# Conditioning stage of a two-layer kernel: work moved from GpSimd and VectorE to ScalarE, output rows accumulated by DMA, last batch reordered

## The chip, the cores and the metric

One core of a Trainium2 chip runs the whole program. The metric is device time in microseconds of one execution, as the median of several runs. Below, PE is TensorE, DVE is VectorE, ACT is ScalarE, POOL is GpSimd and SP is SyncE, which only issues DMAs.

## The reference, cut to what matters

Eight batches of 512 tokens with 256 channels, all in float32.

```python
# layer 0: adapter + layer norm, 8 experts that each choose 128 tokens of a batch; then x = x + layer0
# layer 1, conditioning of every batch (E = 256 channels, D = 8 time constants):
ctx    = causal_ema(x, tau_ctx)                       # h = alpha*h + b over the tokens
gated  = x * sigmoid([x, ctx] @ Wg.T + bg)
mod    = 0.5 + sigmoid(gelu(x @ Wn1.T + bn1) @ Wn2.T + bn2)
traces = causal_ema(gated * mod_d, tau_d) for d in 0..7
temporal = sum_d traces_d * softmax(blend)_d
gate   = sigmoid(temporal @ Wtemp.T + btemp)
soma   = gelu(x @ Wsoma.T + bsoma)
z      = layernorm((soma * gate) @ Wout.T) * gamma + beta
# layer 1, feed-forward on z:
probs  = softmax(z @ router.T)                        # 64 experts, top 8, weights divided by their sum
routed = sum over the chosen experts of weight * (silu(z@Wg_e) * (z@Wu_e)) @ Wd_e   # 128 slots each
shared = (silu(z@Wsg) * (z@Wsu)) @ Wsd
out    = x + routed + shared
```

## The kernel before, in words

Each engine runs its own program, and the engines wait for each other on counting semaphores. `level(m)` is the count at which item m is done. The order on each engine is written out by hand.

Up to about 520 us the kernel does layer 0. Its POOL adds the results, row by row with indirect DMAs, into a DRAM tensor `x1_rows` that began as a copy of x. From 520 us to about 855 us it runs the conditioning as a pipeline over the batches: `conditioning` calls `step(b)` for b from -1 to 9. Step b works on the traces of batch b, on the gate, the output product and the layer norm of batch b-1 and on the routing and the shared feed-forward of batch b-2, and prepares batch b+1. From about 857 us the 64 routed experts follow.

The units that the change and the prediction touch:

- `weighted(b, d)` (ACT) scales the gated input by a blend weight; `drive_of(b, d)` (POOL, L635) multiplies it by the modulation; `scan_unit(b, d)` (DVE, L1271) runs the moving average over it; `add_trace(b, d)` adds the result to a sum, on POOL (L643) for d = 1, 2, 3, 5, 6, 7 and on DVE (L1280) for d = 4 (and for d = 6, 7 of the last batch). There are three drive buffers and three trace buffers.
- `temp_in` (PE), `gate_out` (ACT, L936), `gate_soma` (DVE) and `out_in` (PE, L1714) follow on the finished sum. `stats` (DVE) takes mean and variance, `rstd_of` (POOL, L621 to L626) makes the scale and shift, `normalise` (ACT, L945) writes four tiles of `zrow`, and `z_in` (PE, L1722) transposes them.
- On PE a step is: `x1T_in(b+1)`, `shared_b_in(b-2)`, `logits_in(b-2)`, `h1_in(b+1)`, `temp_in(b-1)`, `shared_a_in(b-2)`, `t8_in(b+1)`, `out_in(b-1)`, `wg_in(b+1)`, `down_in(b-2)`, `z_in(b-1)`, `soma_in(b+1)`.
- `pick` (DVE) finds the eight largest logits, and writes the mask `mask_all` (L1335). `route_weights` (DVE) divides the chosen exponentials by their sum and puts them behind the 256 channels in `zrow`. `z_store` (SP) writes `zrow` to `z_rows`.
- `shared_b`, `shared_a`, `down_in` are the shared feed-forward. `finish` (DVE, L1370) halves it and adds x, which `row_in` (SP) has loaded from `x1_rows`; `row_store` (SP, L454) writes `out`.
- `prep(k, part)` turns `mask_all` into the token numbers (`slots`, L1409) of experts 4k to 4k+3. Experts 0 to 3 are prepared in `last_share`, that is, in step 9.
- In the expert stage POOL issues for each expert a gather of 128 rows of `z_rows` (L721) and a scatter that adds 128 result rows to `out` or `odd_rows` (L728), all in one order. At the end one DMA adds `odd_rows` to `out` (L745).
- `turn(n, count)` (PE, L1601) multiplies constants into an unused PSUM bank.

## Time and profile before

| | us |
|---|---|
| median of 3 runs | 1121.03 |
| lowest and highest run | 1117.95, 1122.76 |
| the profiled execution, its own time | 1116.69 |
| its span, first to last instruction | 1114.9 |
| layer 0 | 0 to about 520 |
| conditioning, batches 0 to 7 | about 520 to 856 |
| routed experts | about 857 to 1091 |
| last accumulation of `odd_rows` | 1091 to 1115 |

Over the span PE is busy 86%, DVE 67%, ACT 41% and POOL 60%. A share of busy time is an average over stages that have different limits, so the stages have to be read one by one. The profiled execution was 4.3 us faster than the median.

### The profile page before, as it was taken

How to read it: one execution, taken by the hardware profiler on the slowest of the kernel's cores; microseconds unless marked ns; L12 is line 12 of the kernel's file. 1: busy time of each engine (PE TensorE's matmuls, PEld its weight loads, DVE VectorE, ACT ScalarE, POOL GpSimd, SP SyncE). 2: the span in 40 equal slices, each digit the busy share in tenths (PEclk: the TensorE clock that was granted, in tenths of full speed). 3: DMA queues.
4: the chain of work that ended last, by engine and by line, in shares of the span. 5: the costliest groups of instructions: out<-in, count | busy, mean ns of one | idle time of the engine just before them, and what ended most of it. 6: DMA issues, size and time to landing. Idle time of an engine off the chain costs nothing.

```text
span 1114.9 us, 14811 instructions
## 1 busy us (share of the span) xinstructions
PE 954.6 (86%) x4524; PEld 668.5 (60%) x4524; DVE 743.1 (67%) x1522; ACT 461.2 (41%) x835; POOL 664.1 (60%) x496
## 2 busy tenths in 40 slices
PE   4968999999999999987379899988586899999960
PEld 2533698899989998863144555544353565556640
DVE  3648566667666766524779999999955786777620
ACT  1330444554455545533455665666421232222320
POOL 2113444555455544407999999999931477777870
PEclk9989999999999999988689999999887799999995
DMA  5869234444354432223212752335168599997557
GB/s 174 281 231 352 58 76 118 90 87 99 76 122 90 92 88 39 30 85 76 96 66 70 240 157 86 91 118 182 44 229 274 143 270 256 257 262 150 91 75 157
DMA packets 89782, 155.46 MB, mean 139 GB/s; under 512 B 12072, under 2 KB 70128, under 8 KB 86576
## 3 DMA queue, kind: packets, MB, share of 16 engines
q1 hardware_dynamic: 48112, 91.27, 25.2%
q0 software_dynamic: 25104, 39.86, 20.6%
q10 hardware_dynamic: 16496, 23.49, 6.2%
q8 instruction: 32, 0.52, 0.2%
q14 instruction: 38, 0.31, 0.1%
HBM read 119.56 MB, written 43.42 MB: 146 GB/s over the span
## 4 chain that ended last, share of the span: by engine, by line
POOL 13%; PE 10%; issue 10%; DMA 9%; DVE 4%; ACT 2%; POOLq 2%; DVEq 1%; ACTq 0%; SPq 0%
DMA odd_rows<-ys,slots 5%; POOL wide L635 4%; PE bank L1662 4%; POOL wide L643 3%; DMA xg<-z_rows,slots 2%; POOL xg L721 2%; POOL out L728 2%; POOL odd_rows L728 2%; DVE wide L1271 1%; PE bank L1739 1%; PE bank L1729 1%; PE bank L1722 1%; ACT zrow L945 1%; DMA z_rows<-zrow 1%; ACT wide L895 1%
## 5 line engine op out<-in xcount | busy, mean ns | idle before, releaser
L635 POOL TENSOR_TENSOR wide<-wide 128x1024 f32<-128x1024 f32 x64 | 156.6, 2461 | 30.8 <-issue 30.6
L1271 DVE TENSOR_TENSOR_SCAN wide<-bank,wide 128x512 f32<-128x512 f32 x128 | 149.3, 1209 | 22.8 <-POOL wide L635 22.6
L871 ACT ACTIVATE h_raw<-bank,b 128x512 f32<-128x512 f32 x128 | 88.1, 689 | 168.1 <-PE bank L1635 165.7
L1208 DVE TENSOR_TENSOR h_lo<-h_raw,h_hi 128x512 fp32r<-128x512 f32 x128 | 87.3, 692 | 91.8 <-ACT h_hi L875 91.8
L1650 PE MATMUL bank<-w_hi,h_hi 128*128 128x256 f32 x512 | 144.4, 282 | 0.1
L1650 PE MATMUL bank<-w_lo,h_hi 128*128 128x256 f32 x512 | 142.1, 278 | 0.0
L1650 PE MATMUL bank<-w_hi,h_lo 128*128 128x256 f32 x512 | 142.0, 277 | 0.0
L609 POOL DMA_INDIRECT x_rows<-ob,put x64 | 110.3, 1723 | 28.3 <-issue 16.0
L643 POOL TENSOR_TENSOR wide<-wide 128x1024 f32<-128x1024 f32 x46 | 108.5, 2359 | 11.9 <-issue 8.1
L895 ACT ACTIVATE wide<-wide,blend 128x512 f32<-128x512 f32 x128 | 84.2, 715 | 59.3 <-POOL wide L635 55.5
L1635 PE MATMUL bank<-ex_hi,w_hi 128*128 128x512 f32 x256 | 99.5, 389 | 2.4 <-issue 2.4
L1635 PE MATMUL bank<-ex_hi,w_lo 128*128 128x512 f32 x256 | 100.8, 394 | 0.0
L1635 PE MATMUL bank<-ex_lo,w_hi 128*128 128x512 f32 x256 | 100.4, 392 | 0.0
L1650 PEld LDWEIGHTS bank<-w_hi,h_hi 128*128 128x128 f32 x512 | 96.9, 189 | 1.6 <-issue 1.1
L721 POOL DMA_INDIRECT xg<-z_rows,slots x64 | 63.5, 993 | 57.0 <-DMA z_rows<-zrow 25.9
L1650 PEld LDWEIGHTS bank<-w_lo,h_hi 128*128 128x128 f32 x512 | 96.9, 189 | 0.3 <-issue 0.2
L1650 PEld LDWEIGHTS bank<-w_hi,h_lo 128*128 128x128 f32 x512 | 96.7, 189 | 0.0
L603 POOL COPY put<-idxT 128x4 int32<-128x4 int32 (+1 forms) x16 | 3.0, 187 | 132.2 <-DVE ob L1197 132.2
L589 POOL DMA_INDIRECT xg<-n_rows,take x60 | 64.4, 1074 | 26.1 <-issue 13.7
L875 ACT ACTIVATE h_hi<-h_raw 128x512 fp32r<-128x512 f32 x128 | 77.9, 621 | 0.0
L728 POOL DMA_INDIRECT odd_rows<-ys,slots x32 | 51.4, 1606 | 20.0 <-DMA odd_rows<-ys,slots 9.7
L1042 ACT ACTIVATE sg<-bank 128x192 f32<-128x192 f32 x64 | 21.2, 331 | 100.4 <-PE bank L1887 100.4
(239 smaller groups left out, 2041.3 us busy)
## 6 DMA issues: line engine op xcount, KB each, us to landing
wide<-in_mwp SPq DMA_DIRECT2D x40, 512.0 KB, 4.5
wide<-m_rows SPq DMA_DIRECT2D x16, 1024.0 KB, 4.9
w1s<-in_fW SPq DMA_DIRECT2D x8, 1024.0 KB, 5.4
w2s<-in_fW SPq DMA_DIRECT2D x8, 1024.0 KB, 5.3
own<-in_mwp SPq DMA_DIRECT2D x15, 512.0 KB, 4.4
z_rows<-zrow SPq DMA_DIRECT2D x8, 640.0 KB, 7.4
head<-in_mwp SPq DMA_DIRECT2D x9, 512.0 KB, 4.5
xT<-in_xT ACTq DMA_DIRECT2D x8, 512.0 KB, 4.2
```

The lines of the kernel that those rows point to most:

```text
L609: G.indirect_dma_start(x1_rows[:, :], bass.IndirectOffsetOnAxis(ap=put[p][:, j:j + 1], axis=0), ob[p][:, j, :], None, compute_op=ALU.add). ...
L635: G.tensor_tensor(drive[n % DRIVES], gb[d % 2], md[d // HD][:, d % HD, :].unsqueeze(1).to_broadcast([P, CT, S]), ALU.mult).then_inc(c_u, 1)
L643: G.tensor_tensor(acc[b % 2][:, :, :], acc[b % 2][:, :, :], trace[((D - 1) * b + d - 1) % TRACES], ALU.add).then_inc(c_add, 1)
L721: G.indirect_dma_start(xg1[i][:, :], None, z_rows[:, :], bass.IndirectOffsetOnAxis(ap=slots[:, e:e + 1], axis=0)).then_inc(e_got[i], 16)
L728: G.indirect_dma_start((out, odd_rows)[e % 2][:, :], bass.IndirectOffsetOnAxis(ap=slots[:, e:e + 1], axis=0), ys[e % 6][:, :], None, compu ...
L871: A.activation(h1_raw[f % 4][:, :], bank[:, 2 + f % 4, :], ACT.Gelu_apprx_tanh, bias=b1_0[:, bass.ds(e, 1), f]).then_inc(b_h, 1)
L875: A.activation(h1_hi[:, f - 1, :], h1_raw[(f - 1) % 4][:, :], ACT.Copy).then_inc(b_hi, 1)
L895: o = A.activation(gb[d % 2][:, c, :], gated2[b % 2][:, c, :], ACT.Copy, scale=blend[:, c, d:d + 1])
L1208: V.tensor_tensor(h1_lo[:, f, :], h1_raw[f % 4][:, :], h1_hi[:, f, :].bitcast(F32), ALU.subtract).then_inc(b_lo, 1)
L1271: o = V.tensor_tensor_scan(dst[:, c, :], decay[:, d:d + 1].to_broadcast([P, S]), drive[(D * b + d) % DRIVES][:, c, :], 0.0, ALU.mult, ALU.add)
L1635: o = T.matmul(bank[:, 2 + f % 4, :], w[q][:, at], x[p][:, c, :], start=(c == 0 and n == 0), stop=(c == CT - 1 and n == 2))
L1650: o = T.matmul(rows4(6)[:, j, :], x[:, f, rows], w[q][:, f * H:(f + 1) * H], start=(f == 0 and n == 0), stop=(f == FT0 - 1 and n == 2))
```

## The change

Eight things are done. (1) x and the results of layer 0 are now put into `out` itself; the shared part is added to it by an accumulating DMA that POOL issues (`rows_add`), so that `row_in`, `row_store` and the load of x are gone. The halving of the shared part moves from DVE (`finish`) to ACT (`share_out`). (2) Traces 3 and 5 are added on DVE to traces 4 and 6 (`pair_traces`), and POOL adds the pairs; POOL has five adds for a batch, not six, and DVE two, not one. (3) Two small operations of `rstd_of` move to ACT (`moments`). (4) For all batches but the last, the mask is made by two ACT operations (`chosen_out`). (5) `route_weights` no longer divides; it stores the reciprocal as one more column of `z_rows` (324 columns now, not 320), and the expert stage multiplies. (6) The last batch's rows of `z_rows` go in two transfers from POOL (`last_rows`), first the 256 channels, then the 68 others. (7) In `last_share` the slots of experts 0 to 3 come ahead of the shared feed-forward. (8) PE runs `turn` at three places of the last two steps.

```diff
-ZW = H + E1
+ZW = H + E1 + 4
+        PAIRED = (4, 6)
+        SUMS = tuple(d for d in range(1, D) if d + 1 not in PAIRED)
@@ SP: row_in, row_store and their calls removed; c_load reads out, not x1_rows @@
@@ POOL @@
             def rstd_of(q):
-                pool.wait_ge(c_mv, level(q))
+                pool.wait_ge(c_mw, level(q))
                 pool.wait_ge(c_no, level(q - 1, TT))
-                G.tensor_scalar(veps1[:, :], mv1[:, :, 1], 4 * EPS, None, ALU.add)
-                G.tensor_scalar(shift1[:, :], mv1[:, :, 0], -1.0, None, ALU.mult)
-                pool.drain()
+            def last_rows(part):
+                pool.dma_start(z_rows[(B - 1) * S:TOK, part].rearrange("(t p) c -> p t c", p=P), zrow[:, :, part]).then_inc(z_last, 16)
+            def rows_add(q):
+                pool.wait_ge(c_fin, level(q))
+                pool.dma_start(out[q * S:(q + 1) * S, :].rearrange("(t p) c -> p t c", p=P), ost[:, :, :],
+                               accum_op=ALU.add).then_inc(c_ost, 16)
...
             for e in range(ROWS):
                 e_gather(e)
-            pool.wait_ge(c_ost, level(B - 1, 16))
+            rows_add(B - 1)
+            wait_moved(pool, c_ost, B - 1, 16)
@@ ACT @@
+            def moments(q):
+                act.wait_ge(c_mv, level(q))
+                act.wait_ge(c_no, level(q - 1, TT))
+                A.activation(veps1[:, :], mv1[:, :, 1], ACT.Copy, bias=4 * EPS)
+                A.activation(shift1[:, :], mv1[:, :, 0], ACT.Copy, scale=-1.0).then_inc(c_mw, 1)
+            def chosen_out(q):
+                act.wait_ge(c_top, level(q))
+                A.activation(rep[:, :, :], rep[:, :, :], ACT.Sign, bias=far[:, :], scale=-1.0)
+                act.drain()
+                A.activation(mask_all[:, :, q * TT:(q + 1) * TT].rearrange("p e t -> p t e"), rep[:, :, :], ACT.Relu).then_inc(c_ma, 1)
+            def share_out(q):
+                act.wait_ge(c_dm, level(q))
+                wait_moved(act, c_ost, q - 1, 16)
+                A.activation(ost[:, :, :], rows4(down_bank(q)), ACT.Copy, scale=0.5).then_inc(c_fin, 1)
                 if ahead(b + 1):
                     wg_out(b + 1)
+                if on(b - 2):
+                    share_out(b - 2)
                 if on(b - 1):
                     normalise(b - 1)
@@ DVE @@
+            def pair_traces(b, d):
+                n = (D - 1) * b + d - 1
+                dve.drain()
+                V.tensor_tensor(trace[n % TRACES], trace[n % TRACES], trace[(n - 1) % TRACES], ALU.add).then_inc(c_pair, 1)
+                dve.drain()
@@ last_share, DVE @@
                 pick(B - 1)
-                shared_b(B - 1)
                 prep(0, 1)
                 route_weights(B - 1)
                 prep(0, 2)
-                shared_a(B - 1)
+                shared_b(B - 1)
                 prep(0, 3)
                 prep(1, 0)
-                finish(B - 1)
+                shared_a(B - 1)
                 prep(1, 1)
@@ PE @@
                 down_in(B - 2)
+                turn(6, 2)
                 z_in(B - 1)
             def last_share():
+                turn(1, 2)
                 logits_in(B - 1)
                 shared_b_in(B - 1)
+                turn(1, 2)
                 prep(0, 0)
```

First place: ACT's instructions at the end of a step in the middle of the conditioning, before. L895 is `weighted`, L918 to L924 `t8_out`, L907 `wg_out`, L945 `normalise`, L952 `z_out`.

```order
L895 ACTIVATE wide<-wide,blend 128x512 x2
L918 ACTIVATE wide<-bank,bn_h 8x512
L921 ACTIVATE wide<-wide 8x512
L924 DMA m_rows<-wide 8x512
L895 ACTIVATE wide<-wide,blend 128x512 x2
L907 ACTIVATE bank<-bank,bg_h 128x512 x2
L945 ACTIVATE zrow<-bank,shift_b,rstd_b 128x256 x4
L895 ACTIVATE wide<-wide,blend 128x512 x4
L952 ACTIVATE zT<-bank,bet,gam 128x512 x2
```

The same place after (L903 is `weighted`, L950 and L951 `moments`, L915 `wg_out`, L993 `share_out`, L959 `normalise`, L966 `z_out`):

```order
L903 ACTIVATE wide<-wide,blend 128x512 x2
L926 ACTIVATE wide<-bank,bn_h 8x512
L929 ACTIVATE wide<-wide 8x512
L932 DMA m_rows<-wide 8x512
L903 ACTIVATE wide<-wide,blend 128x512 x2
L950 ACTIVATE veps<-mv_b 128x4
L951 ACTIVATE shift_b<-mv_b 128x4
L915 ACTIVATE bank<-bank,bg_h 128x512 x2
L993 ACTIVATE ost<-bank 128x1024
L959 ACTIVATE zrow<-bank,shift_b,rstd_b 128x256 x4
L903 ACTIVATE wide<-wide,blend 128x512 x4
L966 ACTIVATE zT<-bank,bet,gam 128x512 x2
```

`moments` stands ahead of `wg_out`, and `share_out`, which waits for `down_in`, stands between `wg_out` and `normalise`.

Second place: POOL's whole period in the middle of the conditioning, before. L635 is `drive_of`, L643 `add_trace`, L621 to L626 `rstd_of`.

```order
L621 TENSOR_SCALAR veps<-mv_b 128x4
L622 TENSOR_SCALAR shift_b<-mv_b 128x4
L624 TENSOR_TENSOR rstd_b<-veps,mhalf 128x4
L626 TENSOR_TENSOR shift_b<-shift_b,rstd_b 128x4
L635 TENSOR_TENSOR wide<-wide 128x1024
L643 TENSOR_TENSOR wide<-wide 128x1024
L635 TENSOR_TENSOR wide<-wide 128x1024 x2
L643 TENSOR_TENSOR wide<-wide 128x1024 x2
L635 TENSOR_TENSOR wide<-wide 128x1024
L643 TENSOR_TENSOR wide<-wide 128x1024
L635 TENSOR_TENSOR wide<-wide 128x1024 x2
L643 TENSOR_TENSOR wide<-wide 128x1024 x2
```

The same after (L626 is `drive_of`, L637 `add_trace`, L615 and L617 `rstd_of`, L644 `rows_add`), from `rstd_of` to the last add of the period:

```order
L615 TENSOR_TENSOR rstd_b<-veps,mhalf 128x4
L617 TENSOR_TENSOR shift_b<-shift_b,rstd_b 128x4
L626 TENSOR_TENSOR wide<-wide 128x1024 x2
L644 DMA out<-ost 128x4x256
L626 TENSOR_TENSOR wide<-wide 128x1024
L637 TENSOR_TENSOR wide<-wide 128x1024 x2
L626 TENSOR_TENSOR wide<-wide 128x1024
L637 TENSOR_TENSOR wide<-wide 128x1024
L626 TENSOR_TENSOR wide<-wide 128x1024 x2
L637 TENSOR_TENSOR wide<-wide 128x1024
L626 TENSOR_TENSOR wide<-wide 128x1024 x2
L637 TENSOR_TENSOR wide<-wide 128x1024
```

An add and two small operations are gone, and a DMA issue is new; the add of trace 4 stands right ahead of the next `rstd_of`.

Third place: POOL between the last batch's statistics and the first scatter, after (L640 is `last_rows`, L728 the gathers, L735 a scatter). Before, the gathers stood alone, behind a wait for SP's transfers.

```order
L617 TENSOR_TENSOR shift_b<-shift_b,rstd_b 128x4
L640 DMA z_rows<-zrow 128x4x256
L644 DMA out<-ost 128x4x256
L640 DMA z_rows<-zrow 128x4x68
L728 DMA xg_0<-z_rows,slots 128x324
...
L728 DMA xg_5<-z_rows,slots 128x324
L644 DMA out<-ost 128x4x256
L728 DMA xg_0<-z_rows,slots 128x324
L728 DMA xg_1<-z_rows,slots 128x324
L735 DMA out<-ys,slots 4224x256
```

The last `rows_add`, and the wait for its landing, stand behind six gathers and ahead of the seventh and of the first scatter.

## Rows read from the trace of the kernel before

**Rows 1.** Busy time of each engine in two stretches; PEclk is the granted clock's share.

```profile
core 0: us, PE busy (x) PEld busy (x) DVE busy (x) ACT busy (x) POOL busy (x), PEclk, DMA share, GB/s
604.40:641.60 37.20, 34.41 (x115) 19.18 (x114) 35.41 (x54) 23.89 (x38) 35.81 (x19) 0.95 0.65 197
...
820.00:850.00 30.00, 25.35 (x86) 15.12 (x84) 14.46 (x42) 6.57 (x12) 2.73 (x8) 0.83 1.00 341
```

**Rows 2.** Chain that ended last, one period: start, length, what.

```profile
609.31 4.84 POOL wide L635 x2
...
618.06 1.48 ACT zrow L945 x3
...
639.04 2.36 POOL wide L635
```

**Rows 3.** PE: `z_in` of batches 0 and 5 (timeline), and its waits from 604 to 754 us.

```profile
581.95 1.97 PE L1722 MATMUL bank<-ident,zrow 128*128 128x128 f32 x8 [4.93 <-ACT zrow L945]
...
768.86 1.09 PE L1722 MATMUL bank<-ident,zrow 128*128 128x128 f32 x8 [1.72 <-ACT zrow L945]
...
PE bank L1722 <- ACT zrow L945: 9.3, 4, 2.6
```

**Rows 4.** ACT timeline: `normalise`, `weighted` and a copy from PSUM.

```profile
654.68 1.93 ACT L945 ACTIVATE zrow<-bank,shift_b,rstd_b 128x256 f32<-128x256 f32 x4 [2.27 <-POOL shift_b L626]
656.50 2.56 ACT L895 ACTIVATE wide<-wide,blend 128x512 f32<-128x512 f32 x4
...
665.30 1.02 ACT L902 ACTIVATE head<-bank 128x1024 f32<-128x1024 f32 x1
```

**Rows 5.** POOL timeline: drives, a small operation and an add.

```profile
572.24 5.63 POOL L635 TENSOR_TENSOR wide<-wide 128x1024 f32<-128x1024 f32 x2
577.85 0.24 POOL L621 TENSOR_SCALAR veps<-mv_b 128x4 f32<-128x4 f32 x1
...
656.67 2.38 POOL L643 TENSOR_TENSOR wide<-wide 128x1024 f32<-128x1024 f32 x1 [0.16 <-issue]
...
771.39 4.67 POOL L635 TENSOR_TENSOR wide<-wide 128x1024 f32<-128x1024 f32 x2
```

**Rows 6.** DVE timeline: an add of two traces beside a POOL instruction.

```profile
572.46 3.21 DVE L1280 TENSOR_TENSOR wide<-wide 128x1024 f32<-128x1024 f32 x1 [0.40 <-POOL wide L643]
```

**Rows 7.** POOL's direct accumulating DMA, and landing times of `row_store` (L454).

```profile
1090.71 1.16 POOL L745 DMA_DIRECT2D out<-odd_rows  x1 [2.71 <-DMA odd_rows<-ys,slots]
...
DMA to landing us min/median/max: 2.9/3.7/10.2
```

**Rows 8.** PE in the last batch: windows, its logits, and `turn` in layer 0.

```profile
834.00:835.00 1.00, 0.00 (x0) 0.00 (x0) 0.00 (x0) 1.00 (x2) 0.00 (x0) 0.69 1.06 342
835.00:836.00 1.00, 0.85 (x4) 0.85 (x5) 0.00 (x0) 0.10 (x1) 0.00 (x0) 0.50 0.96 353
...
835.15 3.67 PE L1729 MATMUL bank<-router,zT 128*128 128x64 f32 x16 [1.54 <-ACT zT L952]
...
L1601 PE MATMUL bank<-flip,ident x64: 592/593/1223, 82.8 to 119.0; 128*128 128x512 f32 x64
```

**Rows 9.** DVE timeline of the last batch: first of `pick`, mask copy, slots.

```profile
838.97 0.63 DVE L1324 MAX8 top<-bank 128x8 f32<-128x64 f32 x4 [7.08 <-PE bank L1729]
...
841.14 0.73 DVE L1335 CAST mask_all<-mask 128x256 bf16<-128x256 f32 x1
...
854.26 0.23 DVE L1409 TENSOR_SCALAR slots<-slot_g,dummy_row 128x4 int32<-128x4 f32 x1
```

**Rows 10.** Chain that ended last, into the expert stage.

```profile
846.44 9.74 DMA z_rows<-zrow
...
857.01 4.05 DMA xg<-z_rows,slots
```

**Rows 11.** POOL timeline at the start of the experts.

```profile
872.94 0.95 POOL L721 DMA_INDIRECT xg<-z_rows,slots  x1 [11.03 <-DVE slots L1409]
...
881.09 1.56 POOL L728 DMA_INDIRECT odd_rows<-ys,slots  x1 [1.25 <-DVE xgT L1501]
884.04 1.02 POOL L721 DMA_INDIRECT xg<-z_rows,slots  x1 [1.39 <-DVE slots L1409]
```

More of the change, by code:

```diff
@@ L222, in build @@
         neg = sb("neg", [P, TT, E1])
-        mask = sb("mask", [P, TT, E1])
+        far = sb("far", [P, 1])
         ex = sb("ex", [P, TT, E1])
@@ L482, in c_step @@
                     m_load(b + 1, 0)
-                if on(b - 2) and b != B:
+                if on(b - 2) and b < B:
                     z_store(b - 2)
@@ L608, in b_put_rows @@
                 p = r & 1
-                G.indirect_dma_start(x1_rows[:, :], bass.IndirectOffsetOnAxis(ap=put[p][:, j:j + 1], axis=0),
+                G.indirect_dma_start(out[:, :], bass.IndirectOffsetOnAxis(ap=put[p][:, j:j + 1], axis=0),
                                      ob[p][:, j, :], None, compute_op=ALU.add).then_inc(b_put[p], 16)
@@ L661, in step @@
                     rstd_of(b - 2)
+                if b == B + 1:
+                    pool.wait_ge(c_no, level(B - 1, TT))
+                    last_rows(slice(0, H))
                 if on(b - 1):
                     drive_of(b - 1, 7)
-                if on(b - 1):
-                    add_trace(b - 1, 5)
                 if ahead(b):
                     drive_of(b, 0)
+                if on(b - 3):
+                    rows_add(b - 3)
                 if ahead(b):
@@ L689, in step @@
                     drive_of(b, 6)
+                if on(b):
+                    add_trace(b, 4)
                 if b == B:
@@ L973, in step @@
                     exponentials(B - 2)
+                    chosen_out(B - 2)
                     shared_b_out(B - 2)
@@ L976, in step @@
                     shared_out(B - 2)
+                    moments(B - 1)
                     normalise(B - 1)
+                    share_out(B - 2)
                     return
@@ L1005, in step @@
                     exponentials(b - 2)
+                    chosen_out(b - 2)
                 if on(b):
@@ L1025, in last_step @@
                 shared_out(B - 1)
+                share_out(B - 1)
             def front_only():
@@ L1468, in step @@
                 if on(b):
-                    add_trace(b, 4)
+                    pair_traces(b, 4)
                 if on(b):
@@ L1475, in step @@
                     scan_unit(b, 6)
-                if on(b - 2):
-                    finish(b - 2)
+                if on(b):
+                    pair_traces(b, 6)
                 if on(b):
@@ L1481, in front_only @@
             def front_only():
+                V.memset(zrow[:, :, H + E1 + 1:ZW], 0.0)
+                V.memset(far[:, :], -1.0e38)
                 ctx_scan(0, alpha)
@@ L1741, in shared_b_in, with shared_a_up, shared_a_gate, shared_a_in @@
                 o.then_inc(c_bm, 1)
-            def shared_a_in(q, half=None):
-                if half != 1:
-                    pe.wait_ge(c_hsB, level(q))
-                for n, lo in ((0, 0), (1, 2 * P)):
-                    if half in (None, n):
-                        for c in range(CT):
-                            o = T.matmul(bank[:, 2 + n, :], ws_gu[:, c, lo:lo + P], zT[:, c, :], start=(c == 0),
-                                         stop=(c == CT - 1))
-                if half != 0:
-                    o.then_inc(c_am, 1)
+            def shared_a_up(q):
+                for c in range(CT):
+                    T.matmul(bank[:, 3, :], ws_gu[:, c, 2 * P:3 * P], zT[:, c, :], start=(c == 0), stop=(c == CT - 1))
+            def shared_a_gate(q):
+                pe.wait_ge(c_hsB, level(q))
+                for c in range(CT):
+                    o = T.matmul(bank[:, 2, :], ws_gu[:, c, 0:P], zT[:, c, :], start=(c == 0), stop=(c == CT - 1))
+                o.then_inc(c_am, 1)
+            def shared_a_in(q):
+                shared_a_up(q)
+                shared_a_gate(q)
             def down_in(q):
@@ L1760, in down_in @@
                     pe.wait_ge(c_pad, 1)
-                pe.wait_ge(c_fin, level(q - 1))
+                if q == B - 1:
+                    pe.wait_ge(e_slot, level(0))
+                else:
+                    pe.wait_ge(c_fin, level(q - 1))
+                into = rows4(down_bank(q))
                 for j in range(TT):
-                    T.matmul(rows4(4)[:, j, :], hsA[:, j * P:(j + 1) * P], ws_da[:, :], start=True, stop=False)
-                    o = T.matmul(rows4(4)[:, j, :], hsB[:, j * P:(j + 1) * P], ws_db[:, :], start=False, stop=True)
+                    T.matmul(into[:, j, :], hsA[:, j * P:(j + 1) * P], ws_da[:, :], start=True, stop=False)
+                    o = T.matmul(into[:, j, :], hsB[:, j * P:(j + 1) * P], ws_db[:, :], start=False, stop=True)
                 o.then_inc(c_dm, 1)
```

95 lines of the change are left out of this document (48 added, 47 removed).

## Prediction

> **What bounds the kernel now.** I read the busy time by stretch first, then the chain of waits, then each engine's timeline over one period, and last the stretch from the last batch to the first experts. In a period of the conditioning POOL, DVE and PE are all over nine tenths busy [rows 1], so no single engine is the limit by its share. The chain of waits says which loop is closed: POOL's drives, `rstd_of`, ACT's `normalise`, PE from `z_in` to `temp_in`, ACT's `gate_out` and `weighted`, POOL's next drive [rows 2]. The reader is to see that this loop passes through three engines. PE itself has one real gap in a period, ahead of `z_in`: four such waits sum to 9.3 us, and that of batch 5 is 1.72 us [rows 3]. From `z_in` of batch 0 to that of batch 5 there are five periods, 768.86 - 581.95 = 186.9 us, 37.4 each; without the waits, 186.9 - 9.3 - 1.7 = 175.9 us, PE's own run is 35.2 us a period, all of it back to back but for half a microsecond. So whatever is done for POOL and DVE, a period can't be shorter than 35.2 us plus the wait ahead of `z_in`.
>
> After the last batch the experts wait for one transfer: `z_rows` is issued at 846.44 and takes 9.74 us, the first gather starts at 857.01 [rows 10], though its slots were there at 854.5 [rows 9]. In between the DMA engines are full with expert weights, 341 GB/s [rows 1].
>
> **The change, part by part.** All shifts are against the profiled execution.
>
> *The start, batches 0 and 1.* Up to `rstd_of` of batch 0 POOL does one add less: 2.38 + 0.16 = 2.5 us [rows 5]. DVE does one add more. Such an add has both inputs in SBUF, and the two engines exclude each other: DVE's took 3.21 us because it stood behind a POOL drive [rows 6], and the drives beside it took 5.63 instead of 4.67, so POOL pays 0.96 [rows 5]. The two small operations gone from `rstd_of` are worth 0.24 each and a gap, about 0.6 [rows 5]. `z_in` of batch 0 comes 2.5 - 1.0 + 0.6 = 2.1 us earlier.
>
> *The periods.* POOL's work falls by 2.5 + 0.6, and rises by about 1.0 for the second DVE add and by the issue of `rows_add`. An issue of this kind, direct and accumulating, took 1.16 us [rows 7]; with a gap, 1.3. That leaves a gain of only 0.8 us for POOL in a period of 37.4. But the loop is closed elsewhere. `share_out` stands on ACT ahead of `normalise` and waits for `down_in`; `down_in` is PE's last work before `z_in`, and `z_in` waits for all of `normalise`. So PE now waits, after `down_in`, for a copy of 1024 PSUM columns, 1.02 us, and for four tiles, 1.93 us [rows 4], 3.0 us with the hand-overs, however early POOL is. Before, `normalise` could run beside `down_in`. Five periods become 175.9 + 15.0 = 190.9 us, 38.2 each, 4.0 us more in all. `z_in` of batch 5 stands at -2.1 + 4.0 = +1.9. `chosen_out` and `moments` lie in ACT's idle time (23.9 busy of 37.2 [rows 1]); the work taken off DVE (`finish`, mask copy, division) is hidden too, since DVE isn't in PE's loop; it pays for the second add. If that cover were gone, two adds of up to 3.21 each would put DVE near 38 us, no more than PE's loop.
>
> *Step 7.* Before, the first drive of batch 7 came 2.53 us after `z_in` began (771.39 [rows 5] less 768.86 [rows 3]), since POOL was late; now it can follow `weighted` (half of 2.56 [rows 4]), 1.3 us after: -1.2. From there POOL is the limit. It has as many adds as before up to `rstd_of`, and more by 1.3 for `rows_add` and 1.0 for the DVE add, less 0.6 and some 0.4: +1.3. `z_in` of batch 6 is at +1.9 - 1.2 + 1.3 = +2.0, and so is `z_in` of batch 7, with PE's run between them unchanged.
>
> *The last batch.* The clock granted to PE falls from 2.4 to 1.2 GHz between 834 and 836 us, after a stretch with no matmul, and the logits take 3.67 us [rows 8]; at full clock half of that. The `turn` there fills the wait. One `turn` is two instructions, 0.45 us apart, so two are 1.8 us, 0.3 more than the wait of 1.54 [rows 8]. The logits end at +2.0 - 1.85 + 0.3 = about +0.4, and `pick` starts at 839.4. From there to the slots were 15.5 us [rows 9]; the mask copy (0.73 [rows 9]), the last multiply (0.5), `shared_a` (1.4) and some 0.7 of waits for PE at 1.2 GHz leave that path: 12.2 us, slots at 851.6. The small transfer can be issued at 845.1, 1.3 us earlier than before. When it lands is the open price. Unhindered it takes at the least the 2.9 us of a 512 KB store [rows 7] and the issue, and the slots decide (first gather at 852.4); hindered as before, 9.74 [rows 10], it lands at 855, and behind the two larger transfers that POOL has put into its queue since 836, at the end of the weights, about 856. I take the first gather at 855.0, nearer to the loaded row, -2.0 us. PE is ready for it at about 858, and the gather's 4.05 us [rows 10] end at 859.
>
> The page "DMA: Bandwidth & Descriptors" of the Trainium skill, section "SWDGE vs HWDGE vs iDMA", says that each DMA engine takes turns between the queues fed by software and by hardware; by it the small transfer would pass the weights and the first gather would be near 852.4, a sum 2.6 us lower. By the row of 9.74, where the store stood behind weights in one queue, the gather is at 855.7, 0.7 higher. No row here shows a large POOL transfer beside the weights.
>
> *The experts.* POOL issues gathers 4 and 5, then `rows_add` of batch 7, then waits until it has landed; gathers 6 and 7 and the first scatter are queued behind it. Issue and landing are 1.2 + 3.7 (median; 2.9 to 10.2) [rows 7], 5.0 us. Before, POOL waited here anyway, 1.25 and 1.39 us against a usual 0.3 [rows 11], so 2.0 are absorbed: +3.0 (from +2.1 to +9.4). From there to the last scatter POOL's gaps are mostly the usual 0.3, so the delay stays. The wider rows and the tiny multiply for each expert I cost at nothing: they lie in DVE's idle time.
>
> Sum: -2.0 + 3.0 = +1.0, a profiled time of 1116.7 + 1.0 = 1117.7. The profiled execution was 4.3 below the median of 1121.0, so the median should be 1122.0.
>
> **The rivals.**
>
> *The relief arrives.* If PE's wait isn't the closing one, the period falls by POOL's 0.8 us, or 1.1 where the DVE adds meet POOL between two instructions: five periods -5, the start -2.1, step 7 +1.3, together -6. The last batch gives its 4.0 as above (+2.0 at `z_in`, -2.0 at the first gather), and the hold of POOL costs 1 if two thirds of it are absorbed: -9, 1112. For it: POOL is 96% busy. Against it: the order of ACT, which leaves no other time for `normalise`.
>
> *POOL's DMA issue is dear.* An issue of 128 indirect rows is 0.95 to 1.56 us [rows 11]. If the price goes by rows, 512 rows are 4 to 6 us of POOL in every period. From the first drive to `add_trace` 7, which `temp_in` awaits, POOL has only about 0.5 us to spare, so it decides from 1.9 us an issue. At 4 us: 2.1 in four periods, 2.8 in step 7, +10: 1132. Against it: the 1.16 us of L745 [rows 7], a transfer cut into as many pieces.
>
> *POOL is held longer before the scatters.* A landing near 8 us instead of 3.7, or PE's clock not kept (`turn` at half clock costs 1.8 more, the logits keep their 3.67), is +4: 1126.
>
> **How the numbers follow.** The forecast, 1122, has 0.40; the relief, 1112, 0.28; the dear issue, 1132, 0.14; the longer hold, 1126, 0.18. Half a percent, 5.6 us, is what a measurement can tell from no change: faster is below 1115.4, slower above 1126.6. Faster: 0.25 of the relief and 0.04 of the forecast, 0.29. Slower: 0.14, half of the hold, 0.04 of the forecast, 0.27. Within: 0.44. The range, 1110 to 1131, leaves out the far ends of the first and second rivals. The forecast's own range is 1118 to 1126.
>
> **What would show it.** In the trace after: PE's wait ahead of `z_in` at 2.9 to 3.1 us, released by ACT, and a period of 38.2; POOL idle for 1 to 2 us in each; `rows_add` at 1.2 us; the logits of batch 7 below 2 us; the first gather near 855; POOL idle some 4 us behind the sixth gather. I am wrong if the wait ahead of `z_in` is shorter than 2.5, if an issue takes over 2 us, or if the first scatter isn't later than before.

## The result and the profile after

The changed kernel took 1140.1 us (median of 4 runs, 1138.5 to 1145.0), the kernel before 1119.5 (4 runs beside them, 1117.8 to 1122.8). The ratio is 1.0188, with a 95% interval of [1.0146, 1.0229]: slower by 20.6 us. The forecast was 1122.0, range 1110 to 1131. Medians, here and below, are over all runs and ratios over the fast ones alone; one run of y2 and two of the kernel before were slow, and without the slow one the median of y2 is 1119.0 us.

The profiled execution of the changed kernel took 1138.46 us, with a span of 1136.7; the span before was 1114.9. The granted clock, 0.930 in the mean, is as before, 0.929. So 21.8 us have to be found. The table splits them at events that both kernels have.

| stretch | before | after | difference | forecast |
|---|---|---|---|---|
| start to `z_in` of batch 0 | 581.95 | 578.59 | -3.4 | -2.1 |
| from there to `z_in` of batch 5 | 186.9 | 213.7 | +26.8 | +4.0 |
| from there to `z_in` of batch 7 | 62.95 | 65.84 | +2.9 | +0.1 |
| from there to `pick` of batch 7 | 7.16 | 5.24 | -1.9 | -1.6 |
| from there to the end | 275.9 | 273.3 | -2.6 | +0.6 |

PE's timeline shows `z_in` of batches 1 to 5 of the changed kernel, and answers to [rows 3]:

```profile
617.27 1.97 PE L1765 MATMUL bank<-ident,zrow 128*128 128x128 f32 x8 [3.53 <-ACT zrow L959]
...
666.39 1.09 PE L1765 MATMUL bank<-ident,zrow 128*128 128x128 f32 x8 [3.27 <-ACT zrow L959]
...
709.00 1.97 PE L1765 MATMUL bank<-ident,zrow 128*128 128x128 f32 x8 [3.97 <-ACT zrow L959]
...
751.02 1.97 PE L1765 MATMUL bank<-ident,zrow 128*128 128x128 f32 x8 [4.91 <-ACT zrow L959]
...
792.33 1.97 PE L1765 MATMUL bank<-ident,zrow 128*128 128x128 f32 x8 [4.41 <-ACT zrow L959]
```

`z_in` of batch 0 was at 578.59. The five periods are 38.7, 49.1, 42.6, 42.0 and 41.3 us; before they were about 37.4. The first has no `rows_add` in it. The wait in brackets is the one that the prediction named, ahead of `z_in` and released by `normalise`, 3.3 to 4.9 us where 3.0 was forecast. The five sum to 20.1 us, 5.1 more than forecast, while the five periods are 22.8 us longer than forecast. So it isn't the main loss. The waits of PE from 600 to 760 us in the changed kernel (engine, line waited for, sum, times, longest), name another:

```profile
PE bank L1765 <- ACT zrow L959: 15.7, 4, 4.9
PE bank L1705 <- POOL wide L637: 12.7, 3, 7.8
```

Before the change the second did not occur in these periods (once, 2.25 us, at 781). L1705 is `temp_in`; it waits for the last add of a batch on POOL, L637. So the question is why POOL is late, and POOL's own timeline answers it. These are two places of the changed kernel, where `rows_add` is L644 and `drive_of` L626:

```profile
620.86 1.40 POOL L644 DMA_DIRECT2D out<-ost  x1
621.76 2.90 POOL L626 TENSOR_TENSOR wide<-wide 128x1024 f32<-128x1024 f32 x1
633.06 2.34 POOL L637 TENSOR_TENSOR wide<-wide 128x1024 f32<-128x1024 f32 x1 [8.40 <-issue]
...
669.99 1.33 POOL L644 DMA_DIRECT2D out<-ost  x1
670.85 2.85 POOL L626 TENSOR_TENSOR wide<-wide 128x1024 f32<-128x1024 f32 x1
676.30 2.36 POOL L637 TENSOR_TENSOR wide<-wide 128x1024 f32<-128x1024 f32 x1 [2.60 <-issue]
```

The issue of the DMA takes 1.3 us, as forecast, and the drive behind it starts at once. Then POOL stands still, 8.40 us once and 2.60, 2.78, 2.57 and 2.60 us in the four steps after. "issue" says that the profile knows no releaser: the pair of traces that this add takes was there at 616.9. What the program has ahead of the add, besides waits for semaphores that had been met, is `pool.drain()`, L636. The chain of waits of the changed kernel, here two steps later, has POOL's sequencer (POOLq) at that line, then the drive that was under way, and then 2.78 us of "issue" ahead of the add:

```profile
710.29 0.44 POOL wide L626
...
711.49 2.41 POOLq L636
713.89 2.39 POOL wide L626
716.29 2.78 issue
719.07 2.37 POOL wide L637
```

Last, the view of line L644, cut to these two DMAs, gives the landing of each (the median over all eight is 6.2 us):

```profile
L644 POOL DMA_DIRECT2D out<-ost x1: 1398/1398/1398, 620.9 to 620.9; - x1
...
DMA to landing us min/median/max: 12.0/12.0/12.0
...
L644 POOL DMA_DIRECT2D out<-ost x1: 1329/1329/1329, 670.0 to 670.0; - x1
...
DMA to landing us min/median/max: 6.1/6.1/6.1
```

The first, issued while SP loaded expert weights, lands 12.0 us behind its start, and the add starts 12.2 us behind it; the second lands after 6.1, and its add starts after 6.3. The other three land after 6.3, 6.1 and 6.1, and their adds start after 6.5, 6.3 and 6.3. So the theory (theory 1) is that a drain on POOL lasts until the DMA that POOL has issued has landed. The last batch is read further down, with its experiments.

### The profile page after: what moved, and what is told of

It reads as the page before. It is cut to its first block and busy times, and to the rows that moved or that the text cites. A ratio compares the mean times of both kernels' runs of the same rounds, so it can differ in the third digit from the quotient of the medians.

```text
span 1136.7 us, 14787 instructions
## 1 busy us (share of the span) xinstructions
PE 964.1 (85%) x4536; PEld 671.7 (59%) x4536; DVE 734.2 (65%) x1501; ACT 482.2 (42%) x873; POOL 647.8 (57%) x482
## 5 line engine op out<-in xcount | busy, mean ns | idle before, releaser
L626 POOL TENSOR_TENSOR wide<-wide 128x1024 f32<-128x1024 f32 x64 | 159.0, 2493 | 52.0 <-issue 51.0
L603 POOL DMA_INDIRECT out<-ob,put x64 | 109.9, 1716 | 28.7 <-issue 16.1
L637 POOL TENSOR_TENSOR wide<-wide 128x1024 f32<-128x1024 f32 x38 | 89.3, 2350 | 39.9 <-issue 24.6
L903 ACT ACTIVATE wide<-wide,blend 128x512 f32<-128x512 f32 x128 | 85.1, 725 | 34.0 <-POOL wide L626 27.7
L728 POOL DMA_INDIRECT xg<-z_rows,slots x64 | 63.3, 990 | 43.9 <-issue 16.5
L583 POOL DMA_INDIRECT xg<-n_rows,take x60 | 64.3, 1072 | 26.2 <-issue 13.7
L735 POOL DMA_INDIRECT odd_rows<-ys,slots x32 | 52.9, 1652 | 15.6 <-DMA odd_rows<-ys,slots 7.6
L1705 PE MATMUL bank<-head,wg 128*128 128x512 f32 x128 | 59.4, 619 | 1.6 <-DVE head L1331 1.6
```

Of the source, the lines that this page charges most:

```text
L603: G.indirect_dma_start(out[:, :], bass.IndirectOffsetOnAxis(ap=put[p][:, j:j + 1], axis=0), ob[p][:, j, :], None, compute_op=ALU.add).then ...
L626: G.tensor_tensor(drive[n % DRIVES], gb[d % 2], md[d // HD][:, d % HD, :].unsqueeze(1).to_broadcast([P, CT, S]), ALU.mult).then_inc(c_u, 1)
L637: G.tensor_tensor(acc[b % 2][:, :, :], acc[b % 2][:, :, :], trace[((D - 1) * b + d - 1) % TRACES], ALU.add).then_inc(c_add, 1)
L728: G.indirect_dma_start(xg1[i][:, :], None, z_rows[:, :], bass.IndirectOffsetOnAxis(ap=slots[:, e:e + 1], axis=0)).then_inc(e_got[i], 16)
L735: G.indirect_dma_start((out, odd_rows)[e % 2][:, :], bass.IndirectOffsetOnAxis(ap=slots[:, e:e + 1], axis=0), ys[e % 6][:, :], None, compu ...
L903: o = A.activation(gb[d % 2][:, c, :], gated2[b % 2][:, c, :], ACT.Copy, scale=blend[:, c, d:d + 1])
```

## The experiments

Theory 1 has these rivals: the DMA holds POOL whatever stands behind it; the drain has a fixed price of 2.7 us; and the order of ACT, the prediction's own loop, makes the longer periods. The kernels named x, y and w ran in three groups, each on a chip of its own, and in each the kernel before ran beside them, at 1119.6 to 1120.0 us. A difference of 2 us or less between kernels of two groups says nothing.

**x1: no drain in POOL's adds.** The waits of the adds for semaphores stay.

```diff
@@ POOL, add_trace @@
                 if d > 1:
                     pool.wait_ge(c_add, added(b, SUMS[SUMS.index(d) - 1]))
-                pool.drain()
                 G.tensor_tensor(acc[b % 2][:, :, :], ...
```

> The changed kernel; only the drain at the head of POOL's adds in the conditioning is left out (the semaphore waits of the adds stay). Theory 1 (the drain behind the accumulating DMA lasts until that DMA has landed): POOL's idle time ahead of the add of trace 6 (8.40 us once, 2.6 to 2.8 us four times after) falls below 0.4 us each, the periods from z_in to z_in fall from 40.4-49.1 to about 38, and the time is 1116 to 1122 us. Rival 1 (the DMA itself holds POOL, whatever stands behind it): the idle time stays or moves to the next instruction, 1137 to 1142 us. Rival 2 (the order of ACT, share_out ahead of normalise, makes the longer periods): 1134 or more.

Measured: 1123.7 us, ratio 1.0030 [1.0005, 1.0056]. One line gives back 16.4 of the 20.6 us. POOL's timeline at the same place of this kernel (the lines behind the drain are one lower, L636 is the add and L643 `rows_add`; `drive_of` stays L626) has no idle time in front of two adds:

```profile
619.77 1.41 POOL L643 DMA_DIRECT2D out<-ost  x1
620.67 2.90 POOL L626 TENSOR_TENSOR wide<-wide 128x1024 f32<-128x1024 f32 x1
622.97 5.41 POOL L636 TENSOR_TENSOR wide<-wide 128x1024 f32<-128x1024 f32 x2
```

It is 1.7 us above theory 1's range, and its five periods are 194.5 us (577.75 to 772.25), 38.9 each, where I wrote "about 38". So in the five periods it gives back 19.2 us, more than the idle times ahead of the adds (16.4), since what followed from them goes too; the stretch from `pick` to the end is 8.5 us longer than in the changed kernel, which is taken up further down. The remainder in the periods is followed up in y1 and w1.

**x2: the drain stays, `rows_add` goes ahead of the drive of trace 7.**

```diff
@@ POOL, step @@
+                if on(b - 3):
+                    rows_add(b - 3)
                 if on(b - 1):
                     drive_of(b - 1, 7)
                 if ahead(b):
                     drive_of(b, 0)
-                if on(b - 3):
-                    rows_add(b - 3)
```

> The changed kernel; rows_add stands ahead of the drive of trace 7, so that three drives (about 7.5 us) lie between it and the next drain, not one; the drain stays. Theory 1 (the drain waits for the landing, 6.2 us behind the issue): almost nothing is left of the wait but where weights share the queues, 1119 to 1126 us. Rival 1 (the DMA holds POOL whatever stands behind it): 1137 to 1142. Rival 3 (the drain costs its 2.7 us wherever it stands behind the DMA, being a fixed price and not a wait for the landing): 1137 to 1142 as well, with an idle time of 2.6 us still ahead of the add.

Measured: 1133.1 us, 1.0117 [1.0078, 1.0156], between the two. The place shows why:

```profile
658.51 1.34 POOL L644 DMA_DIRECT2D out<-ost  x1 [2.85 <-DVE wide L1307]
659.38 7.48 POOL L626 TENSOR_TENSOR wide<-wide 128x1024 f32<-128x1024 f32 x3
667.11 2.36 POOL L637 TENSOR_TENSOR wide<-wide 128x1024 f32<-128x1024 f32 x1 [0.25 <-issue]
```

With three drives between the DMA and the next drain, the idle time ahead of the add is 0.25 us, so the drain has no fixed price of 2.7 us. The rest is a new wait: `rows_add` now stands for up to 2.9 us in front of the drive of trace 7, waiting for its input (5.7 and 4.2 us in all from 600 to 785 us). The row puts this wait down to a scan on DVE, but `rows_add` waits only for ACT's `share_out`, which ended at 658.2, 0.3 us ahead of the issue. The five periods are 203.6 us, 9.1 more than in x1, and these waits are 9.9. In this one place two effects are mixed, so the time alone decides nothing.

**x3: SP stores the shared part.** x and layer 0 are left out of the output rows of batches 0 to 6, since only POOL's DMA accumulates.

```diff
@@ SP, step @@
                 if ahead(b + 1):
                     m_load(b + 1, 1)
+                if on(b - 2) and b < B + 1:
+                    row_store(b - 2)      # plain DMA of ost to out
@@ POOL, step @@
-                if on(b - 3):
-                    rows_add(b - 3)
```

> The changed kernel; the halved shared part of batches 0 to 6 is stored by SP with a plain transfer, not added by POOL's DMA, so x and layer 0 are left out of these rows of the output; batch 7 as in the changed kernel. Everything else, the order of ACT, the pairs on DVE, the last batch, stays. Theory 1: no idle time ahead of the add of trace 6, as in the kernel without the drain, and an issue of 1.3 us less on POOL in each period: 1113 to 1121 us. Rival 2 (the order of ACT or the pairs make the loss): 1134 or more.

Measured: 1122.4 us, 1.0021 [0.9990, 1.0051], 1.4 us above the range and 1.3 below x1, within what the runs can tell apart. The drains are all in this kernel, and ahead of the add of trace 6, where POOL now has no DMA under way, the idle time is 0.16 us in each period. The five periods, 195.2 us, are about as in x1.

**x4: the kernel before, with the store of the output rows issued by POOL.** Nothing else of the change.

```diff
@@ POOL of the kernel before, step @@
                 if ahead(b):
                     drive_of(b, 0)
+                if on(b - 3):
+                    row_store(b - 3)      # the plain DMA that SP issued
                 if ahead(b):
                     drive_of(b, 1)
```

> The kernel before; only the store of the output rows of batches 0 to 6 is issued by POOL (a plain transfer, no accumulation), between the drives of traces 0 and 1, where the changed kernel has rows_add. Theory 1 (a drain waits for any DMA that POOL has issued): an idle time of 1 to 3 us ahead of the next add and 1.3 us of issue in each of six periods, 15 to 27 us, so 1134 to 1147 us. Rival 4 (only an accumulating DMA is slow to land and holds the drain, a plain one lands in 3.7 us, behind the drive of 2.9 us): 6 times 1.3 plus less than 1, so 1124 to 1131. Rival 2 (POOL's DMA costs nothing that matters): 1118 to 1122.

Measured: 1133.2 us, 1.0125 [1.0073, 1.0177], +13.6 us, just under theory 1's range and above rival 4's. Both were right in part. The store is issued by L647 and lands in 4.5 us in the median, not 6.2; the one in this place lands after 4.0:

```profile
667.42 0.88 POOL L647 DMA_DIRECT2D out<-ost  x1
668.33 2.38 POOL L635 TENSOR_TENSOR wide<-wide 128x1024 f32<-128x1024 f32 x1
671.91 2.35 POOL L643 TENSOR_TENSOR wide<-wide 128x1024 f32<-128x1024 f32 x1 [1.21 <-issue]
```

It lands at 671.4, and the add starts at 671.9. The first store of this kernel lands after 8.5 us, and its add starts after 8.7; for the other three with an add behind them it is 4.5 and 4.6, 3.4 and 3.6, 5.9 and 6.1. Plain or accumulating, the drain waits for the landing; the accumulating one lands later. Moving one cheap issue from SP to POOL costs the kernel before two thirds of what the whole change cost.

**y4: x1 with one drain right behind `rows_add`.**

```diff
@@ POOL, rows_add @@
                                accum_op=ALU.add).then_inc(c_ost, 16)
+                if q < B - 1:
+                    pool.drain()
```

> The kernel without the drain in POOL's adds, with one drain right behind rows_add in the six steps of the conditioning that have it. Theory 1 (a drain lasts until POOL's DMA has landed, 6.0 us behind its start): the drive of trace 1 starts 6 us behind the start of rows_add, not 0.9, five idle times of 4 to 5 us and one longer where weights share the queues, and the time is 1145 to 1158 us. Rival 3 (a drain behind a DMA has a fixed price of 2.7 us): the drive starts 3.5 to 4 us behind, 1132 to 1140.

Measured: 1155.5 us, 1.0345 [1.0312, 1.0377], 31.8 above x1. The next drive starts 677.08 - 670.90 = 6.2 us behind the DMA, which lands after 5.9, so the rival of a fixed price is out:

```profile
670.90 1.33 POOL L643 DMA_DIRECT2D out<-ost  x1
677.08 2.34 POOL L626 TENSOR_TENSOR wide<-wide 128x1024 f32<-128x1024 f32 x1 [4.86 <-issue]
```

Where the same drain stands three drives later (x2) it costs 0.25 us, one drive later 2.6, at once 4.9. That settles theory 1.

**y1: x1 with `share_out` behind `normalise`.** This tests the loop that the prediction had named, for the remaining 3.6 us.

```diff
@@ ACT, step @@
-                if on(b - 2):
-                    share_out(b - 2)
                 if on(b - 1):
                     normalise(b - 1)
+                if on(b - 2):
+                    share_out(b - 2)
```

> The kernel without the drain in POOL's adds (1123.7 us), with share_out moved on ACT from ahead of normalise to behind it. Theory 2 (the prediction's loop: PE can't start z_in before a copy of 1.0 us and normalise of 1.9 us have followed down_in): PE's wait ahead of z_in falls from 3.1-3.7 us to about 2.0-2.5, as in the kernel before, five periods from 194.5 to about 188, and the time to 1116 to 1120 us. Rival 5 (normalise waits for rstd_of and its statistics anyway, so the copy ahead of it costs nothing): the waits stay at 3.1 us or more, 1121 to 1126.

Measured: 1124.0 us, 1.0036 [1.0018, 1.0055]: no gain. The wait ahead of `z_in` even grew, to 4.39 us at batch 3. The time is in rival 5's range, but rival 5 names the wrong thing; this is the place, with L617 the end of `rstd_of`, L452 the store of `z_rows` and L441 `m_load`:

```profile
685.45 0.32 SPq L441 DMA_DIRECT2D wide<-m_rows  x1
685.87 0.39 SPq L452 DMA_DIRECT2D z_rows<-zrow  x1
...
691.14 0.20 POOL L617 TENSOR_TENSOR shift_b<-shift_b,rstd_b 128x4 f32<-128x4 f32 x1 [0.23 <-issue]
...
693.73 1.93 ACT L958 ACTIVATE zrow<-bank,shift_b,rstd_b 128x256 f32<-128x256 f32 x4 [4.58 <-issue]
```

`rstd_of` is done at 691.3, and `normalise` starts 2.4 us later with no releaser named. It overwrites `zrow`, so it also waits for the landing of the last batch's store, which this time took 7.8 us: 685.87 + 7.8 = 693.7. The store is short, but it stands right behind `m_load`, 1 MB, in SP's queue.

**w1 and w2: the store of `z_rows` ahead of `m_load`, alone and with y1.** Both are x1 with

```diff
@@ SP, step @@
+                if on(b - 2) and b < B:
+                    z_store(b - 2)
                 if ahead(b + 1):
                     m_load(b + 1, 0)
-                if on(b - 2) and b < B:
-                    z_store(b - 2)
```

> The kernel without the drain in POOL's adds (1123.7 us), with the store of z_rows issued by SP ahead of the first m_load of a step, not behind it. Theory 10 (normalise waits for the landing of the store of the batch before, 7.6 us behind its issue since the store stands behind 1 MB of m_rows in SP's queue): the store lands in 4 to 5 us, but share_out, 1.0 us, which stands ahead of normalise, then closes the loop, so a small gain alone, 0.2 to 0.5 us a period, 1120 to 1123.5 us. Rival 11 (the landing isn't what normalise waits for): no gain, and a later m_load costs 0 to 4 us, 1124 to 1128.

> As the last, and with share_out moved on ACT behind normalise. Theory 10 with the prediction's loop behind it: only with both out of the way can normalise start when rstd_of is done, about 1.7 us earlier; PE's wait ahead of z_in falls from 3.1-3.7 to 1.5-2.3 us, the period from 38.9 to 37.2-37.8, the time to 1113 to 1118 us. Rival 11: the waits stay above 3, 1122 to 1128. Rival 12 (POOL's or DVE's own chain closes the period at once behind it): the wait ahead of z_in shrinks but the period doesn't, 1121 to 1125.

Measured: w1 1120.3 us, 1.0001 [0.9979, 1.0023]; w2 1115.3 us, 0.9967 [0.9949, 0.9985]. The store lands in 4.3 us in the median in both. PE's wait at batch 3 in w1, and in w2 with what ends it (L992 is `share_out`):

```profile
693.59 1.24 PE L1764 MATMUL bank<-ident,zrow 128*128 128x128 f32 x8 [2.94 <-ACT zrow L958]
```

```profile
688.21 1.93 ACT L958 ACTIVATE zrow<-bank,shift_b,rstd_b 128x256 f32<-128x256 f32 x4 [1.75 <-POOL shift_b L617]
690.02 1.04 ACT L992 ACTIVATE ost<-bank 128x1024 f32<-128x1024 f32 x1
690.19 1.09 PE L1764 MATMUL bank<-ident,zrow 128*128 128x128 f32 x8 [1.55 <-ACT zrow L958]
```

In w1 all five waits are 2.94 us, 14.7 together, and the five periods 191.4 us. In w2 the periods are 187.6 us, 37.5 each, as before the change. So two closing waits of nearly equal length lay over each other, and taking one away (y1) showed nothing.

**w4: the kernel before, with the store ahead of `m_load`.** The edit is that of w1, in the kernel before.

> The kernel before, with nothing but the store of z_rows moved ahead of the first m_load of a step on SP. Theory 10 (the landing closed the loop before the change too: normalise started 0.8 us behind rstd_of's end there): normalise starts within 0.3 us of rstd_of's end, the period falls from 37.4 by 0.5 to 0.8 us, 1114 to 1117 us. Rival 11: 1118 to 1123.

Measured: 1117.6 us, 0.9986 [0.9965, 1.0007], between the two ranges and not to be told from no change. The mechanism is there: in the three steps from 610 to 695 us `normalise` starts 0.03 us behind the end of `rstd_of`, where it was 0.5 to 0.9 before, and the store lands in 3.7 us. But the five periods are 186.3 us against 186.9, where 2.5 to 4 less was expected. Before the change this wait was at most a small part of the loop.

**y2: x1 with the last batch's `rows_add` behind the fourth gather.**

```diff
@@ POOL, start of the experts @@
             for e in range(ROWS):
+                if e == 4:
+                    rows_add(B - 1)
                 e_gather(e)
-            rows_add(B - 1)
```

> The kernel without the drain in POOL's adds, with the last batch's rows_add issued behind the fourth gather, not behind the sixth, so that it has landed before the fifth gather has its slots. Theory 6 (the wait for its landing holds gathers 6 and 7 and the scatters, and the experts never give it back): the idle time of 5.1 us behind it goes to below 0.5, the first scatter comes 5 to 6 us earlier, and the time falls by 4 to 6 us, to 1118 to 1120. Rival 7 (the hold is absorbed, since the experts wait for other things as well): less than 1.5 us, 1122 to 1125.

Measured: 1119.4 us, 1.0006 [0.9988, 1.0024], 4.3 below x1, though the two intervals overlap. The changed kernel, and behind it y2, at this place (gathers are L728 and L727):

```profile
896.57 0.95 POOL L728 DMA_INDIRECT xg<-z_rows,slots  x1 [0.30 <-issue]
897.52 1.47 POOL L644 DMA_DIRECT2D out<-ost  x1
904.21 1.06 POOL L728 DMA_INDIRECT xg<-z_rows,slots  x1 [5.22 <-DMA out<-ost]
...
910.68 1.00 POOL L728 DMA_INDIRECT xg<-z_rows,slots  x1 [0.30 <-issue]
```

```profile
861.21 1.44 POOL L643 DMA_DIRECT2D out<-ost  x1 [3.58 <-ACT ost L992]
872.37 1.06 POOL L727 DMA_INDIRECT xg<-z_rows,slots  x1 [9.73 <-DVE slots L1451]
...
883.57 1.00 POOL L727 DMA_INDIRECT xg<-z_rows,slots  x1 [1.39 <-DVE slots L1451]
```

In y2 the landing lies inside a wait of 9.73 us that POOL has anyway, for the slots of experts 4 to 7. From the fifth gather to the ninth (the last row of each fence) are 15.4 us in the changed kernel (895.32 to 910.68) and 11.2 in y2; before they were 11.1 [rows 11]. So on POOL the hold costs 4.3 us, and this agrees with the times.

**y3: x1 with the last batch as before.** One store of `z_rows` from SP, the shared part ahead of the slots on DVE and PE, no `turn`.

```diff
@@ DVE, last_share (PE's order in the same way) @@
                 pick(B - 1)
+                shared_b(B - 1)
                 prep(0, 1)
                 route_weights(B - 1)
                 prep(0, 2)
-                shared_b(B - 1)
+                shared_a(B - 1)
                 prep(0, 3)
                 prep(1, 0)
-                shared_a(B - 1)
                 prep(1, 1)
```

> The kernel without the drain in POOL's adds, with the last batch worked off as before the change: one transfer of z_rows from SP, shared part ahead of the slots on DVE and PE, no turns; rows_add of batch 7 stays behind the sixth gather. Theory 8 (the new order brings the first gather forward, but not the first expert on PE, which waits behind the shared part): the first gather comes some 3 us later against pick's start, the first expert's product starts within 1 us of where it was (24.1 us behind pick), and the time is 1121 to 1126. Rival 9 (the last batch's changes are worth the 4 us that the prediction gave them): 1126.5 to 1129.

Measured: 1125.7 us, 1.0047 [1.0013, 1.0082], 2.0 above x1, but the two intervals overlap. The first gather is 861.76 - 842.42 = 19.3 us behind `pick`, against 13.7 in x1; the first expert's product is 23.9 against 24.1. The changed kernel shows the reason in PE's timeline (L1813 and L1814 are `down_in`, L1932 the transposes of the gathered rows):

```profile
878.79 0.70 PE L1813 MATMUL bank<-ws_da,hsA 128*128 128x256 f32 x2 [2.17 <-DVE hsA L1402]
...
883.61 0.59 PE L1814 MATMUL bank<-ws_db,hsB 128*128 128x256 f32 x2
884.13 0.40 PE L1824 MATMUL bank<-tri,mstat 128*32 128x128 bf16 x4
...
885.55 0.41 PE L1932 MATMUL bank<-ident,xg 128*128 128x128 f32 x2
```

The gather was issued at 877.06 and landed 7.0 us later, at 884.1, where the one of before took 4.05 [rows 10]. But the row at 885.55 has no wait for it: PE is in `down_in`, which now stands behind the slots, until 884.2, and in `prep` behind it until it turns to the rows. Before, it did wait for the gather:

```profile
861.15 0.66 PE L1879 MATMUL bank<-ident,xg 128*128 128x128 f32 x2 [3.48 <-DMA xg<-z_rows,slots]
```

So of the 4.4 us by which the gather is earlier behind `pick`, PE's own queue takes nearly all back. A gather that landed at 881.1, after the old 4.05 us, would have found PE in `down_in` as well.

**w3: w2 with y2's edit.**

> As the last, and with the last batch's rows_add issued behind the fourth gather. If the gains add (4.3 us of the earlier rows_add, 6 to 9 of the two moves): 1109 to 1114 us, faster than the kernel before by about 0.5 to 1%. If the two moves bring nothing: 1118 to 1121.

Measured: 1106.7 us, 0.9914 [0.9879, 0.9948]: the best kernel of this study, 2.3 us below the range that I gave, and faster than the kernel before by 0.9%. It keeps all eight parts of the change and differs from it in four places: no drain in POOL's adds, `share_out` behind `normalise`, the store of `z_rows` ahead of `m_load`, and the last `rows_add` two gathers earlier.

## Why the prediction was wrong

**The step that failed** is the price of `rows_add` in a period: "An issue of this kind, direct and accumulating, took 1.16 us [rows 7]; with a gap, 1.3. That leaves a gain of only 0.8 us for POOL". The issue was costed, and what is queued behind it on the same engine was not. Issue and gap were right (1.3 us). The missing term is the drain in the add that follows, which holds POOL until the DMA has landed: 8.40 + 2.60 + 2.78 + 2.57 = 16.4 us in the five periods and 2.60 in step 7. Behind it comes what the forecast's loop didn't have: `temp_in` waits (12.7 us in three steps), PE's granted clock is 0.87 of full speed in the longest period, not 0.95 [rows 1], and the `temp_in` behind its longest wait takes 6.75 us, not 3.70. The sum closes: 5.1 us more of waiting ahead of `z_in` than forecast, 13.2 us ahead of `temp_in` in the five periods, and 4.2 us more of PE's busy time (177.4, before 173.2) make 22.5 of the 22.8 us by which the five periods exceed the forecast. The busy time of each engine in that period, in the columns of [rows 1]:

```profile
617.27:666.39 49.12, 37.51 (x115) 20.61 (x115) 33.98 (x50) 26.62 (x43) 33.27 (x16) 0.87 0.45 138
```

And `temp_in` in PE's timeline, behind its longest wait and behind a short one:

```profile
638.01 6.75 PE L1705 MATMUL bank<-wide,wtemp 128*128 128x512 f32 x8 [7.82 <-POOL wide L637]
...
724.05 3.70 PE L1705 MATMUL bank<-wide,wtemp 128*128 128x512 f32 x8 [1.91 <-POOL wide L637]
```

In its longest period no engine is busy for more than 38 of 49 us: the kernel waits. x1 takes the drain away and gives back 16.4 us; that this is also the sum of the idle times is chance, since it is 19.2 us in the periods less what the last batch and the experts lost.

None of the signs by which the prediction wanted to be told wrong came: the wait ahead of `z_in` was over 2.5 us, no issue took 2 us, and the first scatter was later. The rival of a dear issue (1132; its terms add to +11.2, not +10) looked at the right place, POOL behind the issue, for the wrong reason: the issue took 1.3 us.

The trace before had the warning, in a stretch that the prediction did not read. In step 0 POOL issues scatters of layer 0 and then adds; L643 is the add, with the same drain at its head:

```profile
519.20 1.58 POOL L609 DMA_INDIRECT x_rows<-ob,put  x1 [0.17 <-issue]
520.19 1.13 POOL L709 MEMSET hsB<- 64x512 f32 x1
524.61 2.34 POOL L643 TENSOR_TENSOR wide<-wide 128x1024 f32<-128x1024 f32 x1 [3.29 <-issue]
```

An idle time of 3.29 us with no releaser, behind a POOL DMA, is this wait: that scatter lands after 3.8 us, at 523.0, and in x1, without the drain, the add stands right behind the memset (520.21 and 520.70). Here the drain lasted 1.6 us beyond the landing; what those 1.6 us are, no run shows. The Trainium skill, "Perfetto Trace Analysis", section "DMA Instruction — SWDGE (GPSIMD)", says that such an instruction ends in the profile when its descriptors are written, not when the data has moved. The traces agree: 1.3 us in the row and 6.2 to the landing. What a drain behind it does, neither the row nor the Trainium skill says.

**PE's loop** was right in mechanism and in size, but hidden. The forecast was 190.9 us for five periods, with a wait of 3.0 us each behind `share_out` and `normalise`. w1, with the drain and the store's late landing out of the way, has 191.4 us and five waits of 2.94. In the changed kernel it lay under the drain's delay. The second thing missing from this step is the landing of the last store of `z_rows`, 7.6 us, which in x1 made the periods 194.5 (3.1 us more). The prediction treated `rstd_of` as the only thing that `normalise` waits for beside `down_in`.

**The start** came 3.4 us earlier, not 2.1, and that was luck: the last scatter of layer 0 stood at 516.79 in this execution and at 519.20 before (519.22 in x1, with the same layer 0), so 2.4 us come from there. From that scatter on the gain is 1.0 us. The price of a DVE add was about right here: up to `z_in` of batch 0 three `pair_traces` took 3.43, 2.14 and 3.15 us (forecast 3.21), two drives beside one of them took 5.62, and POOL's last add ahead of `rstd_of` waited 1.25 us for the pair, a wait that the sum didn't have. In the periods it was too high: there most `pair_traces` took 1.22 to 1.28 us.

**The last batch.** The logits took 2.00 us, and `z_in` to `pick` fell by 1.9 (forecast 1.6). The path to the slots was 12.6 us from `pick` (forecast 12.2). The small transfer landed 6.6 us behind its issue, and the first gather came 13.7 us behind `pick`, where I had put 15.6. Of the two readings, that the load of the queues holds the transfer, or, by the Trainium skill ("DMA: Bandwidth & Descriptors", section "SWDGE vs HWDGE vs iDMA"), that DMA engines take turns between the two kinds of queue, the second was nearer: in y3 the store in SP's queue, beside the same weights, took 10.9 us. The transfers differ in size, 136 and 648 KB, so the rule is not shown by this. Wrong was the next sentence, "PE is ready for it at about 858, and the gather's 4.05 us [rows 10] end at 859": PE was held by `down_in` and `prep` and came to the first expert 22.1 us behind `pick`, that is 861.5 in the prediction's times, and so the gather's gain of 4.4 us moved the first product by only 0.3 (23.8 to 23.5 us behind `pick`).

**The experts.** The hold of POOL was forecast at +3.0 us, with 2.0 of 5.0 absorbed. The absorbed part was right and the landing was not: from the gather ahead of the DMA to the one behind it are 7.6 us, where 1.26 were usual, 6.4 more and not 5.0 (the DMA landed after 6.4 us, not 4.9); the waits of 1.25 and 1.39 us of [rows 11] are 0.30 now, so about 2.1 us were absorbed; 4.3 remain, which is what y2 gives back. The prediction's rival of a longer hold had this at +4. That the whole stretch from `pick` to the end was still 2.6 us shorter than before I can't explain: in x1 the same stretch is 281.8 us, 8.5 us longer than in the changed kernel with the same code, and in the 200 us that begin 22 us behind `pick` PE's weight loads wait 23.6 us for gathers to land, not 18.3. The stretch is 281.3 us in w2 and 270.3 in w3. So it stays open what part of w3's gain of 8.7 us over w2 is the earlier `rows_add`, which gave only 4.3 over x1.

## What to carry to other kernels

Before a DMA is moved to POOL, look for every drain behind it on POOL: here each lasted until the DMA had landed, so put at least the landing time of work between them, or let the semaphores do the ordering. Cost a moved DMA by its landing and by what is queued behind it, never by its issue alone, and read idle time with no releaser as a question. Where taking one wait away changes nothing, look for a second of the same length under it before giving the first up.

## What the runs showed of the hardware

- A drain on POOL behind a DMA that POOL issued lasted until 0.1 to 0.5 us behind the landing: 6.2 to 6.5 us behind the start of an accumulating one of 512 KB (landed after 5.9 to 6.3), 3.6 to 6.1 us behind the start of a plain one of the same size (3.4 to 5.9), and 12.2 and 8.7 us where expert weights were being loaded. Behind an indirect scatter it lasted 1.6 us beyond the landing. Other POOL instructions behind the DMA were not held; the drive started 0.9 us behind the start of the issue.
- A plain store of 640 or 648 KB on SP's queue landed in 7.2 to 8.2 us behind a load of 1 MB and in 3.7 to 5.0 us ahead of it.
